# A fused two-layer decoder on one core: another ring of PSUM banks, another order of steps and two kinds of copies on another engine in its two softmax attentions

## The chip, the cores and the metric

The kernel runs on one core of one Trainium2 chip. The metric is the device time of one execution in microseconds (us), taken as the median of several runs. A difference of less than about 2% counts as no change.

## What is computed

Four sequences of 256 tokens, 256 wide, pass through two decoder layers of three parts each; each part adds its result to x after a layer norm. The stages are named A to F. A and E are the attentions that the change touches: A has 16 heads of 16 with 4 shared key heads and projections, E has 16 heads over a given context, and no projections.

```python
x = x + _L0_attn_ref(_layernorm(x), ...)                            # A
x = x + _L0_xattn_ref(_layernorm(x), itok, ctx, ctx, ctx)           # B, experts chosen by token
x = x + _L0_ffn_ref(_layernorm(x), ...)                             # C, mixture of experts
x = x + _L1_attn_ref(_layernorm(x), ...)                            # D, state space scan
x = x + _L1_xattn_ref(_layernorm(x), ctx, ctx)                      # E
x = x + _L1_ffn_ref(_layernorm(x), ...)                             # F, mixture of experts

# the heart of A and E, per sequence and head
att = jnp.einsum('bhqd,bhkd->bhqk', q, k) / scale
att = jax.nn.softmax(jnp.where(causal, att, -jnp.inf), axis=-1)
y = jnp.einsum('bhqt,bhtd->bhqd', att, v)
```

## The kernel before, in words

`schedule` writes one list of steps `(kind, stage, index)` for the whole program, by hand. Every engine walks through the same list and issues its own share of each step, so the place of a step in the list is its place on every engine that takes part in it, and each engine is strictly in order. `number` walks the list too and gives each use of a PSUM bank its number in a ring; engines hand banks to each other through a pair of semaphores per ring, `..._full` and `..._read`.

A batch is one sequence of 256 queries, two tiles of 128. An attention makes the scores twice: once with queries on the partitions, in 12 blocks of 128x512 (step `s`, PE lines 1473 to 1484), from which VectorE takes the row maxima (line 1946); and once with keys on the partitions and the maximum already subtracted (step `pv`, PE lines 1510 to 1518), from which ScalarE takes the exponential (line 1143). The queries and keys are bf16 parts of float32 numbers: a number is cut in three, and VectorE makes the cuts in `qkv_split` (lines 1891 to 1918) and `q_rest` (lines 1925 to 1927; the last two of these are plain copies of parts into other slots of the stack). In E `qkv_split` begins with two copies on VectorE, the scaled query (line 1905) and the context (line 1906). `stack_t` turns the stacks on PE (line 1462); ScalarE (line 1126) and VectorE (line 1938) copy the result out. `m_t` turns the maxima on PE (line 1492), ScalarE copies them (line 1133) and a DMA puts them into two rows of the queries.

The loop over a batch b runs k from 0 to 11. Step k issues `s` of batch b+1 and `pv` of batch b, so that the maxima of the next batch are taken beside the exponentials of this one. `pv` also multiplies the exponentials of earlier k with the values (PE line 1537, called values here): the first query tile's at k 1 to 4, the second's at 7, 9 and 11 (twice). Beside these stand, at fixed k:

- at k 4 and 8 the split of one tile of batch b+2 (in A after a product `qkv_mm`, PE line 1448), and one k later its `q_rest`;
- `y_t` of the first tile at k 6, of the second after k 11: ScalarE copies the bank of values out (line 1151), PE turns it (line 1565), VectorE divides by the row sums (lines 1962 and 1966);
- for batch b-1 `o_t` at k 1 (A: PE line 1574, ScalarE line 1157) and `o` at k 3 (A: PE line 1583, VectorE line 1975; both: the residual sum, line 1981), then the layer norm `ln` of the next stage (VectorE lines 1860 to 1874, with a power on GpSimd, line 945, in the middle).

After k 11 come `m_t`, `y_t` and then `stack_t` for batch b+2. Batches 0 and 1 carry two splits each for batches 2 and 3; batches 2 and 3 carry none.

PSUM has eight banks. Score blocks, `qkv_mm`, the odd groups of `stack_t`, `y_t` and `o` share a ring of two banks, V (banks 0 and 1): a block may be written when VectorE has read the block two before it. `pv` and the even groups of `stack_t` have a ring A of three (banks 2, 3, 6). The values of the two tiles take turns in ring O (banks 4 and 5).

In stage B, `b_y` (PE line 1614) adds up in banks 5 and 6.

## Time and profile before

| | |
|---|---|
| time, median of 3 runs (lowest to highest) | 877.12 us (874.18 to 885.82) |
| the profiled execution | 875.9 us, of which the span from first to last instruction is 874.1 us |
| busy in the span | PE 676.2 us, VectorE (DVE) 567.1, ScalarE (ACT) 382.9, GpSimd (POOL) 173.6 |
| mean granted clock of TensorE | 0.888 of full speed |
| stage A | from about 9 to 164 us of the span |
| stage E | from about 610 to 747 us, its first split from 588 us on |

The span is what the profiler saw of one execution. A group line ends with the time its engine stood idle just ahead of it and with what ended that; a line of the waits gives idle time in total, how often and the longest. The page's own chain of work that ended last reaches back only over the last part of stage F and says nothing of A or E. For these the waits, the stretches and the pieces in order of time are of use.

### The profile page before, as it was taken

How to read it: one execution, taken by the hardware profiler on the slowest of the kernel's cores; microseconds unless marked ns; L12 is line 12 of the kernel's file. 1: busy time of each engine (PE TensorE's matmuls, PEld its weight loads, DVE VectorE, ACT ScalarE, POOL GpSimd, SP SyncE). 2: the span in 40 equal slices, each digit the busy share in tenths (PEclk: the TensorE clock that was granted, in tenths of full speed). 3: DMA queues.
4: the chain of work that ended last, by engine and by line, in shares of the span. 5: the costliest groups of instructions: out<-in, count | busy, mean ns of one | idle time of the engine just before them, and what ended most of it. 6: DMA issues, size and time to landing. Idle time of an engine off the chain costs nothing. (4 is left out here: it accounts for less than half of the span.)

```text
span 874.1 us, 16937 instructions
## 1 busy us (share of the span) xinstructions
PE 676.2 (77%) x6016; PEld 497.0 (57%) x6016; DVE 567.1 (65%) x1326; ACT 382.9 (44%) x816; POOL 173.6 (20%) x193
## 2 busy tenths in 40 slices
PE   3657778898768899776787788965578777689997
PEld 2334443464667788664465565544255554578996
DVE  5666654356675456675888898865866655665455
ACT  1024343302255355874575565541144345554553
POOL 5100000121400331016131121211511102203113
PEclk9689996999899899987799898986789796889999
DMA  8700000042112351014000000000033000114433
GB/s 298 257 2 2 1 2 2 0 157 113 48 43 68 127 156 39 18 42 108 2 6 6 6 7 1 12 1 1 0 117 117 23 37 16 53 37 140 139 116 109
DMA packets 39069, 53.09 MB, mean 61 GB/s; under 512 B 9874, under 2 KB 33170, under 8 KB 38558
## 3 DMA queue, kind: packets, MB, share of 16 engines
q1 hardware_dynamic: 35918, 43.62, 15.2%
q0 software_dynamic: 3072, 8.39, 3.1%
q8 instruction: 52, 0.85, 0.4%
q14 instruction: 27, 0.22, 0.1%
HBM read 37.97 MB, written 17.04 MB: 63 GB/s over the span
## 5 line engine op out<-in xcount | busy, mean ns | idle before, releaser
L1143 ACT ACTIVATE s_mega<-bank 128x512 f32<-128x512 f32 x96 | 56.7, 597 | 104.0 <-PE bank L1513 56.2
L1946 DVE TENSOR_REDUCE s_mega<-bank 128x2 f32<-128x512 f32 (+1 forms) x96 | 64.5, 686 | 37.3 <-PE bank L1484 21.1
L2087 DVE TENSOR_TENSOR s_mega<-bank,s_mega 128x176 f32<-128x176 f32 x84 | 28.4, 339 | 78.7 <-ACT s_mega L1183 78.6
L2149 DVE SCALAR_TENSOR_TENSOR s_mega<-s_mega,s_convw 128x256 f32<-128x256 f32 x144 | 67.9, 512 | 1.8 <-ACT s_mega L1245 0.8
L1333 ACT ACTIVATE s_mega<-bank 128x512 f32<-128x512 f32 x64 | 37.5, 602 | 37.5 <-PE bank L1780 37.5
L996 POOL DMA_INDIRECT xd<-s_xn,s_pos x32 | 34.1, 1065 | 94.8 <-issue 94.8
L1183 ACT ACTIVATE s_mega<-bank 128x176 f32<-128x176 f32 x84 | 26.8, 320 | 56.9 <-PE bank L1670 56.7
L945 POOL TENSOR_TENSOR s_rstd<-s_ve,s_mhalf 128x2 f32<-128x2 f32 x24 | 16.8, 699 | 171.6 <-DVE s_ve L1863 171.5
L1680 PE MATMUL bank<-s_ident,s_mega 128*88 128x128 f32 x168 | 34.1, 286 | 21.4 <-DVE s_mega L2087 21.4
L1480 PE MATMUL bank<-s_masks,s_identb 128*128 128x512 bf16 x64 | 29.3, 458 | 26.1 <-DVE s_mega L1946 26.0
L2220 DVE TENSOR_TENSOR s_mega<-s_mega 128x512 f32<-128x512 f32 x64 | 46.8, 735 | 2.4 <-ACT s_mega L1333 2.1
L1006 POOL DMA_INDIRECT s_mega<-yd,s_pos x32 | 31.4, 982 | 73.5 <-DMA yd<-s_mega 59.4
L1111 ACT COPY s_xnT<-bank 128x512 f32<-128x512 f32 x20 | 11.7, 585 | 73.7 <-PE bank L1439 73.4
L1220 ACT COPY s_mega<-bank 128x256 f32<-128x256 f32 x76 | 28.4, 374 | 25.5 <-PE bank L1693 25.1
L1537 PE MATMUL bank<-s_mega 128*32 128x128 f32 x768 | 37.8, 304 | 2.0 <-ACT s_mega L1143 1.3
L1403 PE MATMUL bank<-s_mega 128*32 128x64 f32 x1024 | 29.7, 239 | 12.0 <-DVE s_mega L2220 12.0
L1670 PE MATMUL bank<-s_whF,s_xhF 128*128 (+1 forms) x92 | 34.6, 377 | 4.3 <-DVE s_xlF L2104 2.8
L1403 PEld LDWEIGHTS bank<-s_mega 128*32 128x32 f32 x1024 | 18.7, 117 | 33.8 <-DVE s_mega L2220 17.1
L1680 PEld LDWEIGHTS bank<-s_ident,s_mega 128*88 128x88 f32 x168 | 20.1, 127 | 28.2 <-DVE s_mega L2087 25.1
L1614 PE MATMUL bank<-s_mega 128*128 128x256 f32 x128 | 30.7, 402 | 5.3 <-DVE s_mega L2013 5.3
L1126 ACT COPY s_mega<-bank 96x1024 bf16<-96x1024 bf16 (+1 forms) x32 | 27.0, 908 | 16.3 <-PE bank L1462 16.3
L1705 PE MATMUL bank<-s_xnT,s_mega 128*128 128x256 f32 x96 | 29.6, 436 | 5.3 <-issue 5.3
(276 smaller groups left out, 1928.1 us busy)
## 6 DMA issues: line engine op xcount, KB each, us to landing
s_mega<-xd SPq DMA_DIRECT2D x60, 128.0 KB, 2.1
yd<-s_mega SPq DMA_DIRECT2D x60, 128.0 KB, 1.7
s_wrawF<-in_wF SPq DMA_DIRECT2D x10, 608.0 KB, 6.0
s_wrawC<-in_wC SPq DMA_DIRECT2D x9, 608.0 KB, 10.0
xd<-in_zeros SPq DMA_DIRECT2D x2, 1920.0 KB, 17.4
s_mega<-in_win SPq DMA_DIRECT2D x1, 2112.0 KB, 10.2
s_mega<-in_hots SPq DMA_DIRECT2D x2, 704.0 KB
s_x<-in_x SPq DMA_DIRECT2D x4, 256.0 KB, 5.2
```

Source lines behind the costliest of these rows:

```text
L996: g.indirect_dma_start(xd[i], bass.IndirectOffsetOnAxis(pos[:, i, 2 * t + slot:2 * t + slot + 1], 0), xn[:, b % 2, t % NT, :], None).then_ ...
L1006: g.indirect_dma_start(work[s]["gathered"][k % NGB], None, yd[hf], bass.IndirectOffsetOnAxis(pos[:, hf, m:m + 1], 0)).then_inc(g_in[k % NG ...
L1143: a.activation(PT[:, p % NPT, :], AR[n % 3][:, :], ACT.Exp).then_inc(a_read, 1)
L1333: a.activation(M[k % NM], S[k % 2][:, :], ACT.Exp).then_inc(e_read, 1)
L1403: ins = mm(bk[j * 32:(j + 1) * 32, hg * HS:(hg + 1) * HS], xsp[u % 2][:, hg, j, q].rearrange("p r c w -> p (r c w)"), M[k % NM][:, (2 * j ...
L1537: ins = mm(bk[c32, h4 * P:(h4 + 1) * P], vaug[:, ka % 3, kt, g, :], PT[:, kept[kt] % NPT, (h % 4) * P:(h % 4 + 1) * P], start=(kt == 0), s ...
L1614: ins = mm(Y[b][:, t * D:(t + 1) * D], xm[:, 1, e, k, (b * NT + t) * P:(b * NT + t + 1) * P], ctxT[:, e, k, :], start=(e == 0 and k == 0), ...
L1670: ins = mm(G[n % 2][:, 0:GU], x_[:, k, :], w2[s][w_][:, bass.ds(at_unit + k * GU, GU)], start=(p_ == 0), stop=(p_ == len(parts) - 1))
L1680: ins = tr(HB[n % 2][0:FH, h * P:(h + 1) * P], work[s]["act"][n % 2][:, h * FH:(h + 1) * FH], ident[:, :])
L1946: v.tensor_reduce(nM[:, q, h0:h0 + heads], V[n % 2][:, :].rearrange("p (h k) -> p h k", h=heads), AX.X, ALU.max, negate=True).then_inc(v_r ...
L2149: ins = v.scalar_tensor_tensor(o, raw[:, m % NRAW, h, KS - 1 - k:KS - 1 - k + L], convw[:, ct, KS - 1 - k:KS - k], o, ALU.mult, ALU.add)
L2220: v.tensor_tensor(m, m, CBs[:, u % 2, :, :], ALU.mult).then_inc(m_ready, 1)
```

## The change

- The ring V is used by stage D alone. A and E get a ring W of three banks (0, 1 and 5) for the same uses: a block may be written when the block three before it has been read.
- The values of both tiles go into one bank, 4, with its own semaphore: the first product of a tile waits until ScalarE has copied the tile before it.
- The copy of the values' bank becomes a step `yc`: at k 5 for the first tile and right after `m_t` for the second. `y_t` comes at k 7, and for the second tile behind `stack_t`; for batch 2 behind `pv` 0 of batch 3.
- In A `o_t` stands at k 2 and `o` and the norm at k 4 (behind the split), in E `o` at k 1 and the norm at k 2. The transposes of E's norms for F move from k 7 to 8.
- The two copies of `q_rest` go from VectorE to ScalarE, which waits for the split's parts; the one subtraction stays. `stack_t` waits for both.
- In E a step `q_scale` makes the scaled query and the context copy on ScalarE for batches 1 to 3, one k ahead of the split. Batch 0's stay on VectorE. GpSimd's copy of the context as values no longer waits for VectorE.
- `b_y` in B also waits until all of A's blocks in W have been read.

```diff
@@ schedule
+                steps.extend(("q_scale", s, (1, t)) for t in range(NT) if s == "E" and split_at[t] == k + 1)
...
+                    if s == "E" and k + 1 in LATER_SPLITS and b + 2 < B:
+                        steps.append(("q_scale", s, (b + 2, LATER_SPLITS.index(k + 1))))
...
-                    if k == 1 and b:
-                        steps.append(("o_t", s, b - 1))
-                    if k == 3 and b:
-                        steps.append(("o", s, b - 1))
-                        if s == "A" or b < 3:
+                    if k == 0 and b and b + 1 == B:
+                        steps.append(("y_t", s, (b - 1, 1)))
+                    if s == "A":
+                        if k == 2 and b:
+                            steps.append(("o_t", s, b - 1))
+                        if k == 4 and b:
+                            steps.append(("o", s, b - 1))
+                            norm(s, b - 1)
+                    else:
+                        if k == 1 and b:
+                            steps.append(("o", s, b - 1))
+                        if k == 2 and 0 < b < 3:
                             norm(s, b - 1)
-                    if k == 6:
+                    if k == 5:
+                        steps.append(("yc", s, (b, 0)))
+                    if k == 7:
                         steps.append(("y_t", s, (b, 0)))
-                    if k == (7 if s == "E" else 9) and b and not (s == "E" and b == 3):
+                    if k == (8 if s == "E" else 9) and b and not (s == "E" and b == 3):
                         turn(nxt, b - 1)
...
                     steps.append(("m_t", s, b + 1))
+                steps.append(("yc", s, (b, 1)))
...
-                steps.append(("y_t", s, (b, 1)))
+                if b + 2 < B:
+                    steps.append(("stack_t", s, b + 2))
+                if b + 2 != B:
+                    steps.append(("y_t", s, (b, 1)))
...
-                if b + 2 < B:
-                    steps.append(("stack_t", s, b + 2))
@@ decoder
         V = bank[0:2]
+        W = [bank[0], bank[1], bank[5]]
         AR = [bank[2], bank[3], bank[6]]
+        PO = bank[4]
@@ GpSimd
-                        pool.wait_ge(qk_ready, NT * k + t + 1)
+                        if s == "A":
+                            pool.wait_ge(qk_ready, NT * k + t + 1)
+                        else:
+                            pool.wait_ge(ctx_in, 32)
@@ ScalarE
-                elif kind == "y_t" and s != "D":
+                elif kind == "yc":
...
+                elif kind == "q_scale":
+                    i, t = i
+                    k = attn_index(s, i)
+                    act.wait_ge(ctx_in, 32)
+                    act.wait_ge(xn_ready, ln_index(s, i) + 1)
+                    if k:
+                        act.wait_ge(parts_ready, NT * (k - 1) + t + 1)
+                    a.activation(qf[:, t, 0:D], xn_of(s, i)[:, t, :], ACT.Copy, scale=QSCALE)
+                    a.copy(qf[:, t, D:2 * D], ctxn[:, NT * i + t, :]).then_inc(q_scaled, 1)
+                elif kind == "q_rest":
+                    i, t = i
+                    st = stk[:, t]
+                    act.wait_ge(parts_ready, NT * attn_index(s, i) + t + 1)
+                    a.copy(st[:, 0:NH, 1:4:2, :], st[:, 0:NH, 0, :].unsqueeze(2).to_broadcast([P, NH, 2, HD]))
+                    a.copy(st[:, 0:NH, 2, :], st[:, 0:NH, 5, :]).then_inc(q_copied, 1)
@@ PE
+            def w_bank(*key):
+                n = at["W"][key]
+                if n >= 3:
+                    pe.wait_ge(w_read, n - 2)
+                return W[n % 3]
+
+            def p_bank(*key):
+                if at["P"][key]:
+                    pe.wait_ge(p_read, at["P"][key])
+                return PO
...
                         pe.wait_ge(q_stacked, NT * kk + t + 1)
+                        pe.wait_ge(q_copied, NT * kk + t + 1)
...
-                        pe.wait_ge(o_read, sum(key[1] == "A" for key in at["O"]))
+                        pe.wait_ge(p_read, sum(key[1] == "A" for key in at["P"]))
+                        pe.wait_ge(w_read, sum(key[1] == "A" for key in at["W"]))
@@ VectorE
-                    v.tensor_tensor(st[:, 0:NH, 4, :], r3[:, 0:NH], st[:, 0:NH, 5, :], ALU.subtract)
-                    v.tensor_copy(st[:, 0:NH, 1:4:2, :], st[:, 0:NH, 0, :].unsqueeze(2).to_broadcast([P, NH, 2, HD]))
-                    v.tensor_copy(st[:, 0:NH, 2, :], st[:, 0:NH, 5, :]).then_inc(q_stacked, 1)
+                    v.tensor_tensor(st[:, 0:NH, 4, :], r3[:, 0:NH], st[:, 0:NH, 5, :], ALU.subtract).then_inc(q_stacked, 1)
```

The order of the program, first on PE where batch 0 of A ends. `32x128` out of `s_identb` is `m_t`, `s_zb` is `y_t`, `96x128` is `stack_t`, `s_masks` begins a score block. Before:

```order
L1537 MATMUL bank<-s_mega 32x128 x16
L1492 MATMUL bank<-s_identb,s_mega 32x128 x2
L1565 MATMUL bank<-s_ident,s_zb 128x128 x4
L1462 MATMUL bank<-s_identb,s_mega 96x128 x40
L1473 MATMUL bank<-s_masks,s_identb 128x512
```

And with the change:

```order
L1590 MATMUL bank<-s_mega 32x128 x16
L1545 MATMUL bank<-s_identb,s_mega 32x128 x2
L1515 MATMUL bank<-s_identb,s_mega 96x128 x40
L1618 MATMUL bank<-s_ident,s_zb 128x128 x4
L1526 MATMUL bank<-s_masks,s_identb 128x512
```

The transposes of the stack and those of the values have changed places.

Next ScalarE in a batch of E, from the stack's copies on. `ACTIVATE` into `s_mega` from a bank is the exponential, `s_zb` the copy of the values' bank. Before:

```order
L1126 COPY s_mega<-bank 96x8x128 x4
L1143 ACTIVATE s_mega<-bank 128x512 x7
L1151 COPY s_zb<-bank 128x512
L1143 ACTIVATE s_mega<-bank 128x512 x5
L1133 COPY s_mega<-bank 32x256
L1151 COPY s_zb<-bank 128x512
```

With the change, where `s_xnT` and `s_ctxn` are `q_scale` and `16x2x16` begins the copies of `q_rest`:

```order
L1152 COPY s_mega<-bank 96x8x128 x4
L1169 ACTIVATE s_mega<-bank 128x512 x4
L1185 ACTIVATE s_mega<-s_xnT 128x256
L1186 COPY s_mega<-s_ctxn 128x256
L1169 ACTIVATE s_mega<-bank 128x512 x2
L1191 COPY s_mega<-s_mega 128x16x2x16
L1192 COPY s_mega<-s_mega 128x16x16
L1177 COPY s_zb<-bank 128x512
L1169 ACTIVATE s_mega<-bank 128x512 x2
L1185 ACTIVATE s_mega<-s_xnT 128x256
```

The copy of the values' bank has moved one exponential ahead, and the copies of `q_rest` now stand in front of it.

Last VectorE in batch 1 of A, from the score blocks of k 0 to 3 on; `128x384` begins the split, `128x512` out of a bank is `o`. Before:

```order
L1946 TENSOR_REDUCE s_mega<-bank 128x4 x4
L1975 TENSOR_TENSOR s_mega<-bank,s_mega 128x512
L1981 TENSOR_TENSOR s_x<-s_x,s_mega 128x512
L1860 BN_STATS s_stats<-s_x 128x6 x2
L1862 BN_AGGR s_mv<-s_stats 128x2 x2
L1863 TENSOR_SCALAR s_ve<-s_mv 128x2
L1874 TENSOR_SCALAR s_xn<-s_x,s_mv,s_rstd 128x256 x2
L1946 TENSOR_REDUCE s_mega<-bank 128x2
L1891 TENSOR_TENSOR s_mega<-bank,s_mega 128x384
```

With the change:

```order
L2003 TENSOR_REDUCE s_mega<-bank 128x4 x4
L2003 TENSOR_REDUCE s_mega<-bank 128x2
L1945 TENSOR_TENSOR s_mega<-bank,s_mega 128x384
L1947 TENSOR_TENSOR s_mega<-s_mega 128x320
L1974 CAST s_mega<-s_mega 128x20x16
L1975 TENSOR_TENSOR s_mega<-s_mega 128x320
L1976 CAST s_mega<-s_mega 128x20x16
L1977 TENSOR_TENSOR s_mega<-s_mega 128x4x16
L2032 TENSOR_TENSOR s_mega<-bank,s_mega 128x512
L2038 TENSOR_TENSOR s_x<-s_x,s_mega 128x512
L1914 BN_STATS s_stats<-s_x 128x6 x2
```

The score block of k 4 and the split now stand ahead of `o` and the norm.

## Rows read from the trace of the kernel before

**Rows 1.** Stretches, a batch each, three of A, three of E: us, busy (instructions), clock, DMA.

```profile
55.80:86.90 31.10, 22.48 (x218) 12.20 (x218) 21.24 (x45) 11.38 (x19) 1.73 (x6) 0.95 0.01 2
86.90:118.60 31.70, 23.94 (x235) 14.14 (x236) 20.35 (x47) 12.54 (x21) 2.42 (x7) 1.00 0.01 2
118.60:147.40 28.80, 21.47 (x186) 11.65 (x186) 14.65 (x28) 9.65 (x17) 2.82 (x2) 0.86 0.01 1
639.80:669.00 29.20, 22.50 (x270) 15.16 (x271) 20.66 (x47) 12.23 (x19) 4.29 (x7) 0.88 0.21 74
669.00:700.70 31.70, 23.98 (x274) 16.39 (x274) 21.52 (x48) 12.81 (x20) 4.29 (x7) 0.84 0.23 86
700.70:724.40 23.70, 17.85 (x210) 11.68 (x210) 12.51 (x26) 9.06 (x16) 0.69 (x1) 0.93 0.03 9
```

**Rows 2.** Waits of PE in A's loop, 55.8 to 164.2 us: total, times, longest.

```profile
PE bank L1480 <- DVE s_mega L1946: 8.5, 6, 3.3
PE bank L1565 <- ACT s_zb L1151: 7.1, 6, 1.5
...
PE bank L1448 <- DVE s_mega L1946: 3.4, 1, 3.4
```

**Rows 3.** Waits of PE in E, 610.4 to 747.2 us.

```profile
PE bank L1480 <- DVE s_mega L1946: 12.0, 9, 3.9
PE bank L1565 <- ACT s_zb L1151: 6.4, 6, 1.3
```

**Rows 4.** In order of time, batch 0 of A: start, us, instruction [idle before].

```profile
64.73 2.90 PE L1448 MATMUL bank<-s_mega,s_xnT 128*128 128x384 f32 x4 [3.37 <-DVE s_mega L1946]
...
67.73 0.56 DVE L1891 TENSOR_TENSOR s_mega<-bank,s_mega 128x384 f32<-128x384 f32 x1 [2.56 <-PE bank L1448]
...
70.10 0.23 DVE L1918 TENSOR_TENSOR s_mega<-s_mega 128x64 bf16<-128x64 f32 x1
...
82.83 0.63 PE L1565 MATMUL bank<-s_ident,s_zb 128*128 128x128 f32 x4 [1.02 <-ACT s_zb L1151]
...
84.00 2.89 ACT L1126 COPY s_mega<-bank 96x1024 bf16<-96x1024 bf16 x4 [1.31 <-PE bank L1462]
...
86.95 0.39 PE L1473 MATMUL bank<-s_masks,s_identb 128*128 128x512 bf16 x1 [1.25 <-ACT s_mega L1126]
```

**Rows 5.** VectorE's copies by line and form, 55.8 to 118.6 us: busy, mean ns | idle before.

```profile
L1926 DVE COPY s_mega<-s_mega 128x512 bf16<-128x512 bf16 x4 | 1.1, 284 | 0.0
```

**Rows 6.** VectorE's copies by line and form in E, 639.8 to 700.7 us.

```profile
L1926 DVE COPY s_mega<-s_mega 128x512 bf16<-128x512 bf16 x4 | 1.9, 482 | 0.0
...
L1906 DVE COPY s_mega<-s_ctxn 128x256 f32<-128x256 f32 x4 | 1.1, 284 | 0.0
L1905 DVE TENSOR_SCALAR s_mega<-s_xnT 128x256 f32<-128x256 f32 x4 | 1.1, 282 | 0.0
...
L1927 DVE COPY s_mega<-s_mega 128x256 bf16<-128x256 bf16 x4 | 0.8, 210 | 0.0
```

**Rows 7.** ScalarE's copies of 256 and of 512 columns, whole span.

```profile
L1220 ACT COPY s_mega<-bank 128x256 f32<-128x256 f32 x76 | 28.4, 374 | 25.5 <-PE bank L1693 25.1 <-issue 0.3
...
L1345 ACT COPY s_mega<-bank 128x512 f32<-128x512 f32 x8 | 4.7, 586 | 3.4 <-PE bank L1403 3.4
```

**Rows 8.** In order of time, score blocks of batches 1 and 2 of A.

```profile
99.62 0.38 PE L1480 MATMUL bank<-s_masks,s_identb 128*128 128x512 bf16 x1 [2.32 <-DVE s_mega L1946]
...
131.26 0.38 PE L1480 MATMUL bank<-s_masks,s_identb 128*128 128x512 bf16 x1 [3.32 <-DVE s_mega L1946]
...
134.21 0.63 PE L1480 MATMUL bank<-s_masks,s_identb 128*128 128x512 bf16 x1
```

**Rows 9.** Waits of PE in batch 0 of E, 639.8 to 669 us.

```profile
PE bank L1473 <- DVE s_mega L1946: 1.3, 1, 1.3
```

**Rows 10.** Waits of PE in batch 1 of E, 669 to 700.7 us.

```profile
PE bank L1480 <- DVE s_mega L1946: 3.8, 3, 2.3
PE bank L1565 <- DVE s_mega L1946: 1.8, 1, 1.8
```

More of the change, by code:

```diff
@@ L392, in number @@
 def number(steps):
-    at = {r: {} for r in "TVAOGYRS"}
+    at = {r: {} for r in "TVWAOPGYRS"}
     def fill(ring, *key):
@@ L406, in number @@
         if kind == "qkv_mm" and s == "A":
[L407 removed]
+            fill("W", kind, s, *i)
         if kind == "s":
[L409 removed]
+            fill("W", kind, s, *i)
         if kind == "stack_t":
@@ L709, in decoder @@
         begun_in_d = any(kind == "v_copy" for kind, _, _ in steps)
+        scaled_at = {}
+        for kind, s_, i_ in steps:
+            if kind == "q_scale":
+                scaled_at[s_, i_] = len(scaled_at) + 1
         def ln_index(s, b):
@@ L785, in stack_read @@
             engine.wait_ge(a_full, stack_end(attn_index("A", B - 1), 1) + 1)
-            engine.wait_ge(v_full, at["V"]["stack_t", "A", B - 1, 1, 1] + 1)
+            engine.wait_ge(w_full, at["W"]["stack_t", "A", B - 1, 1, 1] + 1)
             engine.wait_ge(v_copied, NT * B)
@@ L1149, in _ @@
                     if (b, q) > (0, 0):
-                        act.wait_ge(v_full, at["V"]["y_t", s, (b - 1 + q, 1 - q)] + 1)
-                    a.copy(yp[:, :], O[at["O"]["pv", s, b, q] % 2][:, :]).then_inc(o_read, 1)
+                        act.wait_ge(w_full, at["W"]["y_t", s, (b - 1 + q, 1 - q)] + 1)
+                    a.copy(yp[:, :], PO[:, :]).then_inc(p_read, 1)
+                elif kind == "q_scale":
[13 more added lines that the diff above has]
+                    a.copy(st[:, 0:NH, 2, :], st[:, 0:NH, 5, :]).then_inc(q_copied, 1)
                 elif kind == "o_t" and s == "A":
@@ L1420, in _ @@
                         pe.wait_ge(*previous(s))
-                        for ring, read in (("V", v_read), ("A", a_read), ("O", o_read), ("G", g_read),
+                        for ring, read in (("V", v_read), ("W", w_read), ("A", a_read), ("P", p_read), ("O", o_read), ("G", g_read),
                                            ("Y", y_read), ("S", e_read), ("R", r_read)):
@@ L1458, in _ @@
                             heads = 4 if j == 2 and s == "A" else 8
-                            bank_of, full = ((a_bank, a_full), (v_bank, v_full))[j % 2]
+                            bank_of, full = ((a_bank, a_full), (w_bank, w_full))[j % 2]
                             bk = bank_of("stack_t", s, i, t, j)
@@ L1569, in _ @@
                     bk = t_bank("o_t", s, i)
-                    pe.wait_ge(v_read, at["V"]["y_t", s, (i, 1)] + 1)
+                    pe.wait_ge(w_read, at["W"]["y_t", s, (i, 1)] + 1)
                     for d in range(KD):
@@ L1903, in _ @@
                             dve.wait_ge(t_full, at["T"]["lt", "D", B - 1] + 1)
[L1904 to L1907 removed]
+                        if ("q_scale", s, (i, t)) in steps:
+                            dve.wait_ge(q_scaled, scaled_at[s, (i, t)])
+                        else:
+                            dve.wait_ge(xn_ready, ln_index(s, i) + 1)
+                            v.tensor_scalar(qf[:, t, 0:D], xn_of(s, i)[:, t, :], QSCALE, None, ALU.mult)
+                            v.tensor_copy(qf[:, t, D:2 * D], ctxn[:, NT * i + t, :]).then_inc(q_unscaled, 1)
+                            dve.wait_ge(q_unscaled, NT * i + t + 1)
+                    if s == "A":
+                        dve.wait_ge(qk_ready, NT * k + t + 1)
                     if k:
@@ L1958, in _ @@
                     k = attn_index(s, b)
-                    n = at["V"]["y_t", s, i]
-                    dve.wait_ge(v_full, n + 1)
-                    o3 = V[n % 2][:, :].rearrange("p (h w) -> p h w", w=VW)
+                    n = at["W"]["y_t", s, i]
+                    dve.wait_ge(w_full, n + 1)
+                    o3 = W[n % 3][:, :].rearrange("p (h w) -> p h w", w=VW)
                     link(v.reciprocal(rs[:, q, :].unsqueeze(2), o3[:, :, HD:HD + 1]))
@@ L1971, in _ @@
                     if s == "A":
-                        n = at["V"]["o", s, i]
-                        dve.wait_ge(v_full, n + 1)
+                        n = at["W"]["o", s, i]
+                        dve.wait_ge(w_full, n + 1)
                         tmp = y[:, k % 2]
-                        v.tensor_tensor(tmp, V[n % 2][:, :].rearrange("p (t d) -> p t d", t=NT),
-                                        bo[:, :].unsqueeze(1).to_broadcast([P, NT, D]), ALU.add).then_inc(v_read, 1)
-                        dve.wait_ge(v_read, n + 1)
+                        v.tensor_tensor(tmp, W[n % 3][:, :].rearrange("p (t d) -> p t d", t=NT),
+                                        bo[:, :].unsqueeze(1).to_broadcast([P, NT, D]), ALU.add).then_inc(w_read, 1)
+                        dve.wait_ge(w_read, n + 1)
                     else:
-                        dve.wait_ge(v_read, at["V"]["y_t", s, (i, 1)] + 1)
+                        dve.wait_ge(w_read, at["W"]["y_t", s, (i, 1)] + 1)
                     v.tensor_tensor(xb, xb, y[:, k % 2], ALU.add).then_inc(attn_added, 1)
```

70 lines of the change are left out of this document (33 added, 37 removed).

## The prediction

> **What bounds the kernel now.** I read the stretches of the single batches first, then the waits of PE, then the order of time at the longest of them. The stretches [rows 1] show that no engine is full in an attention: in batch 0 of A PE is busy 22.5 of 31.1 us, VectorE 21.2, ScalarE 11.4; batch 1 of E reads nearly the same, 24.0, 21.5 and 12.8 of 31.7. PE and VectorE each do some 21 to 24 us and the batch takes 29 to 32, so they take turns where they should overlap. The waits say how: in A's loop PE stands 8.5 us before score blocks and 3.4 us before a product for the bank that VectorE's row maximum still reads, and 7.1 us before `y_t` for ScalarE's copy [rows 2]; in E 12.0 and 6.4 us [rows 3]. Together that is 37.4 us out of 875.9.
>
> The order of time shows the pattern. With two banks PE is at most two score blocks ahead. When VectorE begins something long, a split from 67.73 to 70.33 [rows 4] or an `o` with its norm, PE runs out of banks. The same happens the other way: PE waits 3.37 us before the product, VectorE then idles 2.56 us for it [rows 4]. At the end of a batch `y_t` waits 1.02 us for a copy that was only just asked for, runs 0.63, and only then come the transposes whose copies ScalarE (idle 1.31 us) must finish before the next score block, which waits 1.25 [rows 4].
>
> **The change part by part.** *The third bank.* It lets PE go one block further, so the first block behind a long VectorE piece is already made, and VectorE finds work when it comes back. I expect the waits for row maxima to go nearly altogether: 2.32 us in batch 1 of A, 3.32 in batch 2 [rows 8], the 3.37 (with VectorE's 2.56) in batch 0 [rows 4]. What is late next is PE's own line or the values.
>
> *The copies taken off VectorE.* In A a tile's two copies are 0.284 us [rows 5] and about 0.21, as the same form in E [rows 6]: 0.50 a tile. In E they are 0.48 + 0.21, and for batches 1 to 3 the scaled query and context 0.28 + 0.28 besides: 1.25 a tile [rows 6]. This counts only where VectorE sets the time, in batches with splits.
>
> *What ScalarE gets.* It has not yet made copies of this form between bf16 slots. Nearest rows: 0.374 us for 256 columns, 0.586 for 512 [rows 7]. A tile's two are so 0.75 to 1.17 us; I take 0.586 + 0.374 = 0.96, by columns. Sixteen tiles: 15.4 us (12.0 to 18.7); six `q_scale` pairs of 2 x 0.374 add 4.5. These 20 us lie in two stages where ScalarE is busy 11 to 13 of some 30 us a batch [rows 1], so the work itself is hidden. If that cover were gone it would cost up to 20 us. Were the strided form much better than the rows, nothing would be gained, since ScalarE's load is not the bound.
>
> The Trainium skill weighs against this edit: "ScalarE: Activation LUTs", section "Rules for kernel authors", puts what is not transcendental on VectorE and budgets some 0.3 us an instruction and 0.83 ns an element on ScalarE. By that, an estimate, a tile's copies would take 0.72 + 0.51 = 1.24 us, some 4.5 us of ScalarE more in all. The trace's 512-column copy of 0.586 [rows 7] is below that figure, and either sum lies in ScalarE's idle time.
>
> What is not hidden is ScalarE's order. `q_rest` now stands in its line ahead of `yc` and of later exponentials, and it waits for VectorE's split. Behind it wait: PE's values of the second tile (one bank, free only when `yc` is done) and the last exponentials. Where the split ends late PE then stands before the values. The bounds are nothing (the split ends before ScalarE comes to it) and a whole split with the copies, 2.60 + 0.96 = 3.6 us a batch. I take 1 to 2 us, between the ends, since of a batch's two splits only the first stands ahead of `yc`, and book it as "new wait" below.
>
> *The batch's end.* With the copy made ahead and the transposes of the stack before `y_t`, ScalarE's stack copies can begin up to 1.3 us sooner (its idle time in [rows 4]); `y_t` then runs beside them. I take 1.3 in A, 1.1 in E.
>
> *One bank for values.* In batches without splits the first product of a tile waits only for a copy of 0.59 us [rows 7]: 0.6 a batch, booked below.
>
> *At nothing:* GpSimd's earlier copy of the context (GpSimd is busy 4.3 of 30 us a batch [rows 1]); `b_y`'s added waits (0.6 us, within the last term of A); the places of `o` and norm, which nobody waits for within the batch, as long as the next stage's weights and turns come later; SP's order, which does not move.
>
> The sum, against the profiled execution:
>
> - A, ahead of the loop: four tiles of copies off VectorE, 4 x 0.50 = 2.0, and half a us of bank waits: -2.5.
> - A, batch 0: idle 2.56, end 1.3, copies 1.0, new wait +0.9: -4.
> - A, batch 1: 2.3 [rows 8], end 1.3, copies 1.0, new wait +1.6: -3.
> - A, batch 2: 3.3 [rows 8], the score's wait at the end 1.25 and some 1.6 from the clock (its mean is 0.86 there [rows 1], and the long wait is what it fell behind), new waits +2.6: -3.5.
> - A, batch 3 into B: two `y_t` waits at the mean of 7.1 / 6 = 1.2 [rows 2], -2.4; values, `y_t` moved behind `pv` and `b_y` +1.9: -0.5.
> - E, ahead of its loop: two tiles of batch 0 save 2 x 0.69, of which 1 us stands in VectorE's path, two of batch 1 save 2 x 1.25 and half a us of waits: -1 and -3.
> - E, batch 0: 1.3 [rows 9], 2 x 1.25, end 1.1, new wait +0.9: -4.
> - E, batch 1: 3.8 + 1.8 [rows 10], new wait +1.1: -4.5 (the copies are inside these waits).
> - E, batch 2: one score wait of (12.0 - 3.8) / 6 = 1.4 and two `y_t` waits of 6.4 / 6 = 1.07 [rows 3], new wait +0.5: -3. Batch 3: 0.
>
> A gives -13.5, E -15.5, together -29.0, so 846.9 for the profiled 875.9; the median lies 1.2 above that execution, so 848 for it. As a check from above: all waits of [rows 2, 3] are 37.4 us, and the forecast takes back about three quarters. If every new wait were at its 3.6 in the six batches with splits or behind them (instead of 7.6 in all), 14 us would be lost: 862. If every new wait were nothing, 840.
>
> **The rivals.** *The clock.* PE's new waits, before the values and before `m_t`, are single and long. After the wait of 3.32 us at 131.26 a score matmul goes from 0.38 to 0.63 us at 134.21, while the 2.32 at 99.62 left batch 1 at 1.00 [rows 8, 1]. So here the longer wait was followed by the lower level, 1.2 GHz, and the shorter one was not. If that happens in six batches, at 0.25 us more for some nine score and exponent blocks each, that is 2.2 x 6 = 13 us: 861. For it: E's batches 0 and 1 are already at 0.88 and 0.84 [rows 1]. Against it: it needs the new waits at their upper bound. The Trainium skill, "TensorE: Matmul & The Clock Gate", section "A second HAM failure mode: psum-queue depth-cycling", describes a clock that goes up and down because PE idles in pieces while it cycles through PSUM banks. By it a third bank should help, the single value bank hurt; that E stands at 0.84 to 0.88 agrees with the first half; no run here shows the second.
>
> *Little change: VectorE paces the loop.* If the waits for banks only show that VectorE is behind, a deeper ring moves the wait and only VectorE's instructions count: 8 x 0.50 in A, 8 x 0.69 + 6 x 0.56 in E, 12.9 us, less the four tiles in batches' slack, about 11: 866. For it: VectorE and PE are busy nearly alike [rows 1]. Against it: VectorE idles 2.56 us at a stretch [rows 4], and 10 of 31 us a batch.
>
> *Slower: ScalarE's line becomes the chain.* At each of the eight splits in the loops, ScalarE waits in order for the split, then copies, then makes `yc` or the exponential that PE and the bank ring of the exponentials wait for: 2.60 + 0.96 + 0.59 = 4.15 us, 8 x 4.15 = 33 lost, and of the 29 + 7.6 gross gain only the copies' 10 or so kept: 877 + 33 - 10 = 900. It decides from the point where VectorE reaches the split later than ScalarE the exponential ahead of it, and PE has no other block with a free bank. Against it: the ring of exponentials has three banks, and a whole k lies between split and `q_rest`.
>
> **How the numbers follow.** The forecast 848 has 0.65; its own range is 838 (new waits nothing and two us of clock more) to 859. The clock rival 0.15, little change 0.14, slower 0.06. The lower end 833 leaves room for the third bank doing more than the listed waits (a clock near 1.00 in E), the upper end 868 takes in the clock and the little change. A measurement of this kernel can tell about 2% from no change: 859.6 and 894.7. The forecast is mostly below the first, the clock rival on it, so faster 0.74, within 2% 0.20, slower 0.06.
>
> **What would show it.** The score blocks' waits for row maxima in A's loop and E should fall from 20.5 us to under 6; `y_t` should no longer wait for ScalarE; ScalarE's stack copies should follow the last copy of the values without 1.3 us idle. Batches should last 27.1, 28.7 and 25.3 us in A and 25.2, 27.2 and 20.7 in E. A new wait of PE, values for ScalarE's `yc`, should appear, 7 to 9 us in all. ScalarE's `q_rest` should take 0.96 a tile. The prediction is wrong if the score waits stay with VectorE full between them (little change), if the clock in the batches of E falls under 0.84 (clock), or if the wait for `yc` and `q_rest` exceeds 25 us (slower).

## The result and the profile after

The changed kernel takes 836.6 us (median of 4 runs, 833.79 to 839.33) where the kernel before takes 877.18 us beside it: a ratio of 0.950 (95% interval 0.946 to 0.954), 40.6 us less. The forecast was 848, with 833 to 868 as its range. The profiled execution took 833.8 us, its span 832.0 (before 874.1); VectorE is busy 553.2 us in it (567.1), ScalarE 398.9 (382.9), PE 665.5 (676.2).

The same stretches as in [rows 1], three batches of A and three of E (us, then busy time and instructions of PE, its weight loads, VectorE, ScalarE, GpSimd; granted clock; DMA share; GB/s):

```profile
51.20:78.70 27.50, 22.34 (x218) 12.78 (x218) 20.46 (x41) 12.69 (x23) 1.73 (x6) 0.93 0.01 2
78.70:106.50 27.80, 23.50 (x234) 14.20 (x234) 19.56 (x43) 13.65 (x25) 2.42 (x7) 1.00 0.01 2
106.50:131.50 25.00, 19.32 (x183) 10.98 (x183) 13.43 (x25) 9.52 (x17) 2.82 (x2) 0.90 0.01 1
...
616.40:638.30 21.90, 19.30 (x271) 13.80 (x271) 17.59 (x38) 14.67 (x27) 3.67 (x7) 1.00 0.17 58
638.30:661.70 23.40, 19.89 (x275) 14.28 (x275) 18.99 (x41) 15.14 (x28) 3.68 (x7) 1.00 0.32 120
661.70:680.40 18.70, 15.52 (x207) 10.37 (x208) 11.85 (x26) 8.90 (x16) 0.69 (x1) 0.98 0.12 46
```

A's batches are 3.6 to 3.9 us shorter, E's 5.0 to 8.3. In E the clock stands at 0.98 to 1.00 where it was 0.84 to 0.93, and PE's busy time for the same matmuls falls from 64.3 to 54.7 us in three batches. Counted along PE, the 20.6 us that these batches lose are 11.0 us of idle time and 9.6 us of busy time.

Waits of PE in A's loop (51.2 to 167.7 us), to set beside [rows 2]:

```profile
PE bank L1618 <- DVE s_mega L2003: 4.0, 2, 2.2
PE bank L1563 <- DMA s_mega<-s_mega: 2.9, 1, 2.9
PE bank L1590 <- ACT s_zb L1177: 2.8, 3, 1.9
...
PE bank L1533 <- DVE s_mega L2003: 1.9, 2, 1.5
```

and in E (595.4 to 703 us), beside [rows 3]:

```profile
PE bank L1545 <- DVE s_mega L2012: 3.9, 1, 3.9
PE bank L1590 <- ACT s_zb L1177: 3.8, 3, 2.2
PE bank L1533 <- DVE s_mega L2003: 2.9, 3, 2.5
PE bank L1563 <- DMA s_mega<-s_mega: 2.9, 1, 2.9
...
PE bank L1618 <- ACT s_zb L1177: 0.8, 1, 0.8
```

Score blocks (line 1533) wait 4.8 us for row maxima where they waited 20.5, and the product's 3.4 us are gone. `y_t` (line 1618) no longer waits for ScalarE, but for 0.8 us. New are the values (line 1590), 6.6 us behind `yc`. Two waits have grown: `y_t` behind VectorE's row maxima in A, 4.0 us for 1.3 (in E its 3.5 are gone), and batch 3's first `pv` (line 1563) behind the DMA of the maxima, 2.9 us in A and in E, which now lacks the cover of `y_t`. Before, this line stood in A's waits and in E's:

```profile
PE bank L1510 <- DMA s_mega<-s_mega: 1.2, 1, 1.2
```

The long wait of `m_t` (line 1545) in E's scoring was there before, with 4.5 us.

The end of batch 1 of E, in order of time (start, us, instruction, idle before):

```profile
657.44 0.57 ACT L1177 COPY s_zb<-bank 128x512 f32<-128x512 f32 x1
...
657.92 3.72 ACT L1152 COPY s_mega<-bank 96x1024 bf16<-96x1024 bf16 x4
...
660.68 0.61 PE L1618 MATMUL bank<-s_ident,s_zb 128*128 128x128 f32 x4
...
661.69 0.39 PE L1526 MATMUL bank<-s_masks,s_identb 128*128 128x512 bf16 x1 [0.41 <-ACT s_mega L1152]
```

ScalarE's stack copies follow the copy of the values without a gap, as against 1.31 us idle [rows 4], and `y_t` runs beside them.

### The profile page after: what moved, and what is told of

Its sections match the earlier page's. It is cut to its first block and busy times, and to the rows that moved or that the text cites. A ratio compares the mean times of both kernels' runs of the same rounds, so it can differ in the third digit from the quotient of the medians.

```text
span 832.0 us, 16954 instructions
## 1 busy us (share of the span) xinstructions
PE 665.5 (80%) x6016; PEld 497.2 (60%) x6016; DVE 553.2 (66%) x1282; ACT 398.9 (48%) x860; POOL 173.7 (21%) x193
## 5 line engine op out<-in xcount | busy, mean ns | idle before, releaser
L2003 DVE TENSOR_REDUCE s_mega<-bank 128x2 f32<-128x512 f32 (+1 forms) x96 | 62.8, 683 | 14.9 <-PE bank L1530 9.0
L2206 DVE SCALAR_TENSOR_TENSOR s_mega<-s_mega,s_convw 128x256 f32<-128x256 f32 x144 | 65.7, 497 | 1.8 <-ACT s_mega L1286 0.8
L1224 ACT ACTIVATE s_mega<-bank 128x176 f32<-128x176 f32 x84 | 26.9, 320 | 56.5 <-PE bank L1724 56.5
L1374 ACT ACTIVATE s_mega<-bank 128x512 f32<-128x512 f32 x64 | 37.4, 602 | 32.1 <-PE bank L1834 32.1
L1734 PE MATMUL bank<-s_ident,s_mega 128*88 128x128 f32 x168 | 34.2, 287 | 21.2 <-DVE s_mega L2144 21.2
L2277 DVE TENSOR_TENSOR s_mega<-s_mega 128x512 f32<-128x512 f32 x64 | 49.0, 768 | 2.6 <-ACT s_mega L1374 2.1
L1032 POOL DMA_INDIRECT s_mega<-yd,s_pos x32 | 31.7, 991 | 74.6 <-DMA yd<-s_mega 61.4
L1590 PE MATMUL bank<-s_mega 128*32 128x128 f32 x768 | 35.6, 289 | 11.8 <-ACT s_zb L1177 6.7
L1734 PEld LDWEIGHTS bank<-s_ident,s_mega 128*88 128x88 f32 x168 | 20.3, 127 | 28.1 <-DVE s_mega L2144 24.9
L1455 PEld LDWEIGHTS bank<-s_mega 128*32 128x32 f32 x1024 | 18.5, 116 | 29.2 <-issue 18.3
L1590 PEld LDWEIGHTS bank<-s_mega 128*32 128x32 f32 x768 | 17.3, 110 | 30.5 <-ACT s_mega L1169 10.3
L1759 PE MATMUL bank<-s_xnT,s_mega 128*128 128x256 f32 x96 | 29.2, 431 | 5.4 <-issue 5.3
L1491 PE MATMUL bank<-s_ident,s_xn 128*128 128x128 f32 x80 | 15.1, 322 | 21.5 <-DVE s_xn L1928 21.5
## 6 DMA issues: line engine op xcount, KB each, us to landing
xd<-in_zeros SPq DMA_DIRECT2D x2, 1920.0 KB, 17.8
```

Source lines behind the costliest of these rows:

```text
L1032: g.indirect_dma_start(work[s]["gathered"][k % NGB], None, yd[hf], bass.IndirectOffsetOnAxis(pos[:, hf, m:m + 1], 0)).then_inc(g_in[k % NG ...
L1374: a.activation(M[k % NM], S[k % 2][:, :], ACT.Exp).then_inc(e_read, 1)
L1455: ins = mm(bk[j * 32:(j + 1) * 32, hg * HS:(hg + 1) * HS], xsp[u % 2][:, hg, j, q].rearrange("p r c w -> p (r c w)"), M[k % NM][:, (2 * j ...
L1590: ins = mm(bk[c32, h4 * P:(h4 + 1) * P], vaug[:, ka % 3, kt, g, :], PT[:, kept[kt] % NPT, (h % 4) * P:(h % 4 + 1) * P], start=(kt == 0), s ...
L1734: ins = tr(HB[n % 2][0:FH, h * P:(h + 1) * P], work[s]["act"][n % 2][:, h * FH:(h + 1) * FH], ident[:, :])
L2003: v.tensor_reduce(nM[:, q, h0:h0 + heads], W[n % 3][:, :].rearrange("p (h k) -> p h k", h=heads), AX.X, ALU.max, negate=True).then_inc(w_r ...
```

## The experiments

Each kernel is the changed one with one part altered, except the two that put one part alone into the old order. Ratios are to the kernel before, run beside it. The stretches are those of one profile each: a batch reaches from its first score block to the next batch's; "A + E" adds the time up to `b_y` in B, E's scoring of batch 0 (beside which batch 1 is split) and its batches 0 to 2, so that B to D, with E's work ahead of its first score block, are left out. No run undoes GpSimd's earlier copy, or the single bank of values alone. Of the single parts only the loss of the third bank is as large as the 2% that count as a change; the smaller effects are read from the intervals and from the stretches.

| kernel | ratio (95%) | A: batch 0, 1, 2 | E: batch 0, 1, 2 | A + E |
|---|---|---|---|---|
| before | 1 | 31.1, 31.7, 28.8 | 29.2, 31.7, 23.7 | 293.8 |
| changed | 0.950 (0.946 to 0.954) | 27.5, 27.8, 25.0 | 21.9, 23.4, 18.7 | 252.6 |
| changed, again | 0.948 (0.944 to 0.953) | 27.5, 28.8, 23.7 | 21.9, 24.3, 18.7 | 253.6 |
| two score banks | 0.973 (0.970 to 0.977) | 29.9, 30.7, 27.6 | 23.7, 23.8, 19.5 | 265.5 |
| copies on VectorE | 0.966 (0.962 to 0.969) | 25.7, 29.1, 25.0 | 25.1, 26.6, 18.7 | 264.6 |
| ring alone | 0.985 (0.979 to 0.991) | 28.2, 32.4, 24.1 | 26.7, 31.7, 20.2 | 275.9 |
| copies alone | 0.987 (0.984 to 0.990) | 31.5, 33.6, 28.1 | 27.9, 30.6, 23.7 | 287.0 |
| `y_t` first | 0.953 (0.947 to 0.958) | 28.7, 30.5, 23.7 | 25.1, 26.5, 18.7 | 260.8 |
| `o`, norm as before | 0.958 (0.954 to 0.963) | 25.7, 29.1, 25.6 | 21.9, 26.5, 20.1 | 253.3 |
| `yc` first | 0.952 (0.948 to 0.955) | 25.0, 29.2, 25.1 | 21.2, 22.7, 18.7 | 248.2 |
| `yc` first, `y_t` later in A | 0.948 (0.942 to 0.953) | 25.0, 27.6, 25.1 | 21.2, 22.7, 18.7 | 246.8 |
| the same, batch 2's `y_t` at its end | 0.947 (0.943 to 0.950) | 26.9, 29.6, 23.5 | 21.2, 22.7, 18.7 | 250.6 |

**How far a stretch can be trusted.** The changed kernel was run once more, unaltered.

> The changed kernel itself, unaltered, beside the others. A and E as in its first profile, 167.7 us to b_y and 84.9 in E's scoring and three batches, each within 0.5; B to D, which the change does not touch, anywhere from 428 to 438. If A and E differ by more than 1 us from the first profile, stage times of single profiles cannot carry the verdicts on the parts.

E repeats: its scoring and three batches take 84.4 us against 84.9. A doesn't within 1 us, 169.2 against 167.7: the expectation failed there. One batch shows what differs. Batch 1 of E in this second profile:

```profile
644.90:669.20 24.30, 21.35 (x274) 15.37 (x274) 19.19 (x41) 15.29 (x28) 3.68 (x7) 0.93 0.32 117
```

The clock is 0.93 where it was 1.00, PE is busy 1.46 us longer and the batch lasts 0.9 us longer. PE's waits in it are those of the first profile, values 2.2 us behind `yc` among them. By the expectation's own rule A's stretches, read from single profiles, cannot carry a verdict on a part; E's can. As a limit drawn from these two profiles, which differ by up to 1.4 us in a batch of A and 0.9 in one of E, differences under 2 us in a batch of A, and under 1 in one of E, are not read as effects below unless several runs repeat them.

**The third bank, taken away.**

```diff
-        W = [bank[0], bank[1], bank[5]]
+        W = [bank[0], bank[1]]
...
-                if n >= 3:
-                    pe.wait_ge(w_read, n - 2)
-                return W[n % 3]
+                if n >= 2:
+                    pe.wait_ge(w_read, n - 1)
+                return W[n % 2]
```

> The changed kernel with the ring W cut to two banks (0 and 1); everything else of the change stays. Ring theory (the third bank carries the gain, because PE no longer stands behind VectorE's long pieces): the terms of the forecast that rest on it are some 19 us, scaled by the measured 41 over the forecast 29 up to 27, so 856 to 864 us, and PE's waits for row maxima are back near 15 to 20 us. VectorE theory (the copies taken off VectorE carry it, the ring only shows VectorE's lag): about 842. Clock theory (E is faster because TensorE stays at its upper level): E's batches fall back under 0.90 here and the loss is mostly in E.

Measured: 854.4 us, 17.8 over the changed kernel's 836.6 and 1.6 below the ring theory's lower end. In A and E together score blocks (line 1533) wait 18.6 us for row maxima, where 15 to 20 was expected. PE's waits in A (52.8 to 177.1 us) are the old ones:

```profile
PE bank L1533 <- DVE s_mega L2003: 8.8, 4, 3.6
PE bank L1500 <- DVE s_mega L2003: 3.4, 1, 3.4
```

In A and E 12.9 us are lost against the first profile of the changed kernel, 11.9 against the second. The profiled executions differ by more, 22.5 us, of which 9.9 lie in B to D, where the edit alters next to nothing (437.6 us against 427.7; the second profile has 434.3). So of the 17.8 some 12 are shown to be the bank's; where the rest comes from is open. The clock theory fails: E's three batches stay at 0.98 to 1.00 and lose only 3 us, although PE waits for row maxima in them again (636 to 703 us; below it batch 1):

```profile
PE bank L1533 <- DVE s_mega L2003: 6.7, 6, 1.5
```

```profile
659.80:683.60 23.80, 19.91 (x275) 14.40 (x276) 18.97 (x40) 15.25 (x28) 3.67 (x7) 1.00 0.32 120
```

The bank is worth most in A.

**The copies, put back on VectorE.**

```diff
-                    a.copy(st[:, 0:NH, 1:4:2, :], st[:, 0:NH, 0, :].unsqueeze(2).to_broadcast([P, NH, 2, HD]))
-                    a.copy(st[:, 0:NH, 2, :], st[:, 0:NH, 5, :]).then_inc(q_copied, 1)
+                    v.tensor_copy(st[:, 0:NH, 1:4:2, :], st[:, 0:NH, 0, :].unsqueeze(2).to_broadcast([P, NH, 2, HD]))
+                    v.tensor_copy(st[:, 0:NH, 2, :], st[:, 0:NH, 5, :]).then_inc(q_copied, 1)
...
-                        steps.append(("q_scale", s, (b + 2, LATER_SPLITS.index(k + 1))))
```

> The changed kernel with both kinds of copies back on VectorE (q_rest's two, and the scaled query and context of E); ring and order stay. Ring theory: only the forecast's copy terms are lost, 8 to 12 us: 845 to 849. VectorE theory: most of the gain goes, 857 or more. If ScalarE's order was what held the changed kernel back (PE's values waiting for yc behind q_rest), the loss is under 5 us: below 842.

846.5 us, 9.9 over the changed kernel: the ring theory's 8 to 12. In the profile 12.0 us lie in A and E, most of it where VectorE makes the copies: 3.1 us in E's scoring, 3.2 in each of E's batches 0 and 1, nothing in batch 2, and 2.9 ahead of A's loop. E's two batches stand at a clock of 0.93 and 0.94 here. Beside the second profile of the changed kernel, whose batch 1 has 0.93 too, batch 1 loses 2.3 us (26.6 for 24.3).

**The ring alone, in the old order.** All of `schedule` as before, the copies on VectorE, with three banks W and the single bank of values.

> The order and the copies of the kernel before, with the three-bank ring W and the single value bank of the change alone. Ring theory: 850 to 858 (19 to 27 below 877). VectorE theory: 870 to 875, the waits for row maxima replaced by waits of PE elsewhere. If the ring needs the other parts to pay: between, about 864.

862.0 us, 15.2 below before (18 in A and E): between "alone" and "needs the other parts". Batch 1 of A and of E are no shorter, 32.4 and 31.7. In A (53.3 to 174.7 us):

```profile
PE bank L1600 <- ACT s_zb L1165: 8.4, 7, 1.5
PE bank L1515 <- DVE s_mega L1987: 3.5, 2, 2.0
```

The score waits (line 1515) are gone but for 3.5 us in A (6.5 stay in E), while `y_t` (line 1600) waits for ScalarE as before: to the same point, `b_y`, it was 8.4 us there too.

**The copies alone.** The old order, two score banks and two of values, with only the copies on ScalarE.

> The order and the banks of before (two score banks, two banks of values, yc at the place of y_t), with only the copies of q_rest, the scaled query and the context on ScalarE. If VectorE's relief counts by itself as much as undoing it cost the changed kernel (10 us): 865 to 869. If it pays only together with the ring and the order: 872 to 877. If ScalarE's line in order becomes the chain (the slower rival of the forecast): over 880.

870.8 us beside 882.1 for before, a ratio that is 11.8 us on 877 and falls into the first case; in A and E the profile shows only 6.8, which falls between the first two. The slower rival is excluded. What ScalarE's order costs is seen in A's loop (53.6 to 183.4 us):

```profile
PE bank L1610 <- ACT s_zb L1168: 12.3, 8, 2.7
PE bank L1525 <- DVE s_mega L1995: 7.2, 4, 3.3
```

`y_t` (line 1610) waits 12.3 us in eight waits, where it waited 8.4 in seven up to the same point before; ScalarE now has the split's copies ahead of it in its line.

**The batch's end: `y_t` ahead of `stack_t` again.**

```diff
-                    if k == 0 and b and b + 1 == B:
-                        steps.append(("y_t", s, (b - 1, 1)))
...
+                steps.append(("y_t", s, (b, 1)))
...
                 if b + 2 < B:
                     steps.append(("stack_t", s, b + 2))
-                if b + 2 != B:
-                    steps.append(("y_t", s, (b, 1)))
```

> The changed kernel with the second tile's transpose of the values (y_t) back ahead of stack_t at a batch's end, and for batch 2 back ahead of batch 3's first step; the copy yc still stands right behind m_t. Order theory (the ends of the batches gave 1.1 to 1.3 us each, and only because the stack's transposes come first): 841 to 844 us, five batch ends longer by 1.1 to 1.6 and ScalarE idle again ahead of its stack copies. Rival (the copy made ahead is enough, y_t then costs only its own 0.63): 838 to 840.

842.2 us by the median, inside the order theory's 841 to 844. But the kernel before took 882.1 beside it; the ratio of 0.953 is 836 on 877, and its interval overlaps the changed kernel's, so whole times don't settle it. E's batches do, 0 and 1 here:

```profile
623.30:648.30 25.00, 20.98 (x270) 15.51 (x271) 18.17 (x39) 14.88 (x27) 3.68 (x7) 0.93 0.31 111
648.30:674.80 26.50, 21.55 (x274) 16.01 (x274) 19.07 (x40) 15.45 (x28) 3.68 (x7) 0.94 0.23 82
```

They take 25.1 and 26.5 us against 21.9 and 23.4: 3.2 and 3.1 lost where 1.1 to 1.6 was expected, with the clock at 0.93 and 0.94 in them. At nearly the same clock, beside the 24.3 us of the second profile, batch 1 loses 2.2. Batch 2 of E is unchanged. In A batch 3's first `pv` waits 1.2 us for the DMA again, so that its 2.9 do come from the moved `y_t`.

**`o` and the norm at their old places.** `o_t` at k 1, `o` and norm at k 3, directly ahead of the split at k 4; E's transposes for F go back to k 7 with them. The first run gave a ratio of 0.955 (0.946 to 0.965). Its profile showed 31.1 us for batch 1 of A and 26.6 for batch 1 of E, and it was run again; the table has the second run.

> The changed kernel with o_t, o, the residual sum and the layer norm back at their k of before (o_t at 1, o and the norm at 3 in both attentions, E's transposes for F at 7). The forecast booked their move at nothing: 835 to 838. Rival (the move is what gave E's batches the gain that the forecast did not have, 3 to 4 us each in batches 0 to 2): 842 to 848, the loss in batches 1 and 2 of E.

> The kernel with o and the norm at their places of before once more. If the loss in batch 1 of A and batch 1 of E (31.1 and 26.6 us in the first profile, 27.8 and 23.4 in the changed kernel) belongs to the placement: both again within 0.5, and 840 to 846 on the whole. If it was a disturbance of that execution: both back under 28.5 and 24, and 835 to 838.

843.8 us (ratio 0.958 against 0.950 and 0.948). Batch 1 of E again takes 26.5 us, batch 2 takes 20.1: 3.1 and 1.4 lost.

```profile
638.40:664.90 26.50, 21.27 (x275) 15.32 (x276) 19.27 (x41) 15.25 (x28) 3.67 (x7) 0.94 0.30 109
```

The clock is 0.94 in batch 1. Beside the 24.3 us that the changed kernel takes at 0.93, 2.2 of the 3.1 are left for the placement. Batch 1 of A gave 29.1, not 31.1, so there the larger loss was not the placement. A as a whole was shorter in this profile, 165.3 us to `b_y` against 167.7 and 169.2, so that A and E together lose nothing in it; it is of the fastest execution, 837.6. The loss in E's batches is shown twice, the 7 us of the whole time by the ratio alone. Batch 1 of E in order of time:

```profile
646.25 0.78 DVE L1923 TENSOR_SCALAR s_xn<-s_x,s_mv,s_rstd 128x256 f32<-128x256 f32 x2 [0.81 <-POOL s_rstd L963]
646.95 0.68 DVE L1998 TENSOR_REDUCE s_mega<-bank 128x2 f32<-128x512 f32 x1
...
647.78 0.38 PE L1528 MATMUL bank<-s_masks,s_identb 128*128 128x512 bf16 x1 [1.64 <-DVE s_mega L1998]
...
649.64 0.62 ACT L1186 COPY s_mega<-s_mega 128x512 bf16<-128x512 bf16 x1 [3.54 <-DVE s_mega L1972]
```

The norm holds up the row maximum of the score block of k 4 and the split behind it; PE stands 1.64 us even with three banks, and ScalarE waits 3.54 us for the split (2.07 in the changed kernel, see the next run) with `yc` behind it.

**`yc` ahead of `q_rest`.**

```diff
+                    if k == 5:
+                        steps.append(("yc", s, (b, 0)))
                     if k - REST in LATER_SPLITS and b + 2 < B:
                         steps.append(("q_rest", s, (b + 2, LATER_SPLITS.index(k - REST))))
...
-                    if k == 5:
-                        steps.append(("yc", s, (b, 0)))
```

> The changed kernel with the copy of the first tile's values (yc) issued ahead of q_rest in the step list at k 5, so that ScalarE need not wait for VectorE's split before it frees the one bank of values. If PE's waits for yc are on the path that sets a batch: 829 to 833, the waits of 6 to 7 us gone. If VectorE is what the batch then waits for: 835 to 837, PE's wait only turns into a later one.

834.3 us, under neither heading and not distinguishable from 836.6. What stood in line in the changed kernel, batch 1 of E:

```profile
648.10 0.62 ACT L1191 COPY s_mega<-s_mega 128x512 bf16<-128x512 bf16 x1 [2.07 <-DVE s_mega L1977]
...
648.63 0.40 ACT L1192 COPY s_mega<-s_mega 128x256 bf16<-128x256 bf16 x1
...
648.93 0.58 ACT L1177 COPY s_zb<-bank 128x512 f32<-128x512 f32 x1
...
649.56 0.64 PE L1590 MATMUL bank<-s_mega 128*32 128x128 f32 x16 [2.22 <-ACT s_zb L1177]
```

With `yc` first the values start at once (batch 0 of E):

```profile
624.60 0.58 ACT L1177 COPY s_zb<-bank 128x512 f32<-128x512 f32 x1
...
625.25 0.62 ACT L1191 COPY s_mega<-s_mega 128x512 bf16<-128x512 bf16 x1
...
625.55 0.64 PE L1590 MATMUL bank<-s_mega 128*32 128x128 f32 x16
```

The waits of 1.09 and 2.22 us (batches 0 and 1) go and the two batches gain 0.7 each, so more than half of it turns into later waits. Two further runs, below, repeat these 0.7.

**A version from these.** `yc` first, and in A the first tile's `y_t` of batches 1 and 2 at k 9; then also batch 2's second `y_t` in A back at the batch's end.

```diff
-                    if k == 7:
+                    if k == (9 if s == "A" and b in (1, 2) else 7):
                         steps.append(("y_t", s, (b, 0)))
```

> The changed kernel with yc ahead of q_rest as in the run before, and with the first tile's y_t of batches 1 and 2 of A at k 9 where it was 7, because PE stood 1.8 to 2.3 us there for a bank that VectorE, busy with o and the norm, had not read. If these waits set batches 1 and 2: 829 to 832 (2 to 3 us under the run with yc ahead alone), batch 1 of A at 26 to 27 us. If VectorE's work sets them: no change from that run, 833 to 835.

> The kernel of the run with yc ahead of q_rest and A's y_t at k 9, and besides in A the second tile's y_t of batch 2 back at the end of batch 2 (in E it stays behind batch 3's first step). From the stages of the runs so far: ahead of b_y 164.7 less 1.3 to 1.6, E's scoring and batches 82.1: 245 to 246 us in A and E, 7 less than the changed kernel's 252.6. On whole times, with B to D alike: 0.990 to 0.993 of the changed kernel run beside it. If B to D vary by more than that between executions, the two medians do not differ, and only the stages do.

835.4 and 833.4 us, ratios 0.948 and 0.947. Neither is told apart from the changed kernel on the whole. For the first, that is the second case of its expectation: batch 1 of A took 27.6 us, and the waits came back ahead of score blocks (line 1533, 6.6 us in A's batches 0 to 2 where `yc` first had 2.2). In E both repeat the 62.6 us that `yc` first took for three batches, against 64.0 and 64.9, a gain of 1.4 to 2.3. In A the second came out at 167.1, not at the 163 that was added up. The 1.3 us that I took for the place of batch 2's `y_t` are explained as well by the clock: the unaltered changed kernel shows 23.7 in its second profile, at 0.98 where the first has 25.0 at 0.90.

## Why the prediction was right, and where it was short

The forecast of a gain, its mechanism and its range held; the gain was 40.6 us where 29 was worked out. Point by point:

- *The third bank* was right in kind: of some 19 us in the terms, 17.8 appear when it is taken away, of which A and E show some 12, and 15.2 when it is put in alone, of which they show 18. The score waits fell to 4.8 us; "under 6" was said.
- *The copies* were right: about 10 us in the terms, 9.9 measured. ScalarE's pair takes 0.617 + 0.400 = 1.02 us (rows below), 0.96 was taken. The 1.24 us that the prediction estimated from the Trainium skill is more than was measured; "ScalarE: Activation LUTs", "Rules for kernel authors", gives that budget for an ACTIVATE whose bias is a pointer operand, not for plain copies. ScalarE's order didn't become the chain. The clock rival went the other way: E's clock rose.
- *The new wait* behind `yc` was right in place and nearly in size: 7 to 9 us was said, 6.6 stand. But it costs less than was booked for it: 0.9 and 1.1 us in batches 0 and 1 of E, where doing away with it gains 0.7 each.
- *A* came out near, 16.7 us (184.4 less 167.7; 15.2 in the second profile) for 13.5: 4.6 ahead of the loop for 2.5, then batch by batch 3.6, 3.9, 3.8 and 0.8 against 4, 3, 3.5 and 0.5.
- *E* is where the sum was short: batches 0, 1 and 2 gained 7.3, 8.3 and 5.0 us, forecast 4, 4.5 and 3, so 9.1 more together. E's scoring gained 3.9 for 3. B to D were 2.9 us shorter and what comes after batch 2 of E 1.9 longer (151.6 us for 149.7), which is no more than these stretches vary: the latter takes 148.4 to 152.5 us in the other runs.

The "check from above" was no bound. The profiled execution gained 42.1 us, more than the 37.4 of all waits listed, since those lists leave out the waits ahead of A's loop, and PE's busy time fell too.

Three steps failed in E. One is a reading: for batch 0 the sum took one wait of 1.3 us [rows 9], and the same view has two more behind row maxima, which are gone in the changed kernel:

```profile
PE bank L1565 <- DVE s_mega L1946: 1.7, 1, 1.7
PE bank L1480 <- DVE s_mega L1946: 1.5, 2, 0.9
```

They are 3.2 us, and batch 0 gained 3.3 more than forecast.

The second is "*At nothing:* ... the places of `o` and norm, which nobody waits for within the batch". Nobody waits for their result, but the split, the row maxima and ScalarE's `q_rest` stand behind them on VectorE; undoing the move (with that of the transposes for F) costs 3.1 + 1.4 us in E, of which 2.2 + 1.4 at an equal or better clock.

The third is the term of the clock. I booked 1.6 us in batch 2 of A and left E's 0.84 to 0.88 as it was, with a better one only in the low end of the range. The sum priced waits only: its 11.5 us for the three batches are close to the 11.0 us of idle time that PE lost in them, and the 9.6 us by which PE's busy time fell for the same matmuls stand in no term. What these are worth can be estimated from the two profiles of the changed kernel: 0.9 us of batch 1 of E for 1.46 us of PE's time, and in batches 1 and 2 of A 1.0 us for 1.7 and 1.4 for 1.4. That is 0.6 to 1 to one, an estimate of 6 us or more of the 9.1. The batch's end belongs to this: sized at 1.1 us from ScalarE's idle time, it cost 3.2 and 3.1 when undone, and PE's busy time rose by 1.7 us with it in either batch (20.98 for 19.30, 21.55 for 19.89).

These steps overlap, since a wait that goes and a clock that rises shorten the same batch; their sum is more than 9.1, and how the 9.1 divides among them is not shown.

That the shorter waits are what keeps the clock up is argued, not shown. For it: a batch of E that lasts 25 us or more has a clock of 0.94 or less in every run (the copies on VectorE, `y_t` first, `o` and norm as before). But a lower clock also makes a batch longer. Against it: with two banks PE waits 6.7 us for row maxima in E's batches and the clock stays at 0.98 to 1.00, and the changed kernel itself shows 0.93 once with the same waits. No run held the waits and varied the clock on purpose, or the other way round.

The parts add up to more than one by one: in E's three batches (84.6 us before) the ring alone gives 6.0, the copies alone 2.4, and the whole 20.6. With two banks all else gives 17.6, with the copies on VectorE 14.2, so the order adds 15.2 us to the copies and 8.2 to the ring; it was not run alone. The copies want `yc` as a step of its own, since otherwise `y_t` stands behind them (12.3 us of waits in A where the copies were put in alone). With the ring alone batch 1 of E stays at 31.7 us; which of the other parts it needs no run tells, but the batch's end is not all of it, since `y_t` first has 26.5 there.

## What to carry to other kernels

When engines wait for each other in turns, price a step that is moved by what stands behind it in its engine's line, not by who needs its result. Where the granted clock of a stretch is below 1, a gain in busy time may come on top of the waits that go, as 9.6 us did here: estimate the stretch a second time with the busy time of its matmuls at the upper level, and give that case a chance of its own, since it follows the waits only loosely. Read the parts of a change in their own stretches, and measure how far the same kernel repeats there before reading differences of a few microseconds.
